# A transformer block with routed experts: softmax maxima and inverses taken off TensorE in the joined stage

## What is computed

```python
x = x + 0.5 * ffn(layernorm(x), ...)
x = x + recurrence(layernorm(x), ...)
x = x + 0.5 * ffn(layernorm(x), ...)

def ffn(x):                      # each of its two parts is residual
    h = layernorm(x) * ln1_w + ln1_b
    q, k, v = split(h @ w_qkv)   # 16 heads of 8 channels
    attn = softmax(q @ k.T / sqrt(8))
    x = x + (attn @ v) @ w_proj
    g = layernorm(x) * ln2_w + ln2_b
    e = argmax(g @ gate_w + gate_b)          # one of 8 experts
    return x + gelu(g @ w1[e]) @ w2[e]
```

## Time and profile before

| | |
|---|---|
| time, median of 3 runs | 1472.45 us (1472.34 to 1479.55) |
| the profiled execution | 1473.18 us, span 1471.4 us |
| TensorE matmul busy | 1230.9 us, 84% |
| VectorE busy | 1042.9 us, 71% |
| ScalarE busy | 860.7 us, 58% |
| GpSimd busy | 553.6 us, 38% |
| mean granted TensorE clock | 0.909 of full |

### The profile page before, as it was taken

How to read it: one execution, slowest core, us unless ns; L and a number is a source line. 1 busy time by engine, 2 the same in 40 slices (tenths; PEclk the granted TensorE clock), 3 DMA queues, 4 the chain that set the end, 5 groups by cost and what they waited for, 6 DMA issues and landing times. The chain is left out here.

```text
span 1471.4 us, 36051 instructions
## 1 busy us (share of the span) xinstructions
PE 1230.9 (84%) x12512; PEld 661.3 (45%) x12513; DVE 1042.9 (71%) x1842; ACT 860.7 (58%) x1742; POOL 553.6 (38%) x797
## 2 busy tenths in 40 slices
PE   2799999999997596398888754999999999993893
PEld 1234444444443596145455442344444444442893
DVE  3889988988992332478788745888898988963232
ACT  2288877778775353444334411588788778881451
POOL 6122324323212354355676536222332431222462
PEclk9599999999999799599999955799999999996896
DMA  4322442222110121100000003122122122100224
GB/s 117 71 74 74 130 121 68 82 71 73 55 36 9 53 67 47 42 2 3 3 2 2 3 1 87 57 75 65 49 82 73 53 81 66 56 15 30 56 66 122
DMA packets 81540, 82.40 MB, mean 56 GB/s; under 512 B 16249, under 2 KB 53724, under 8 KB 81392
## 3 DMA queue, kind: packets, MB, share of 16 engines
q1 hardware_dynamic: 72560, 69.88, 16.7%
q0 software_dynamic: 4608, 8.44, 1.8%
q10 hardware_dynamic: 4224, 2.10, 0.5%
HBM read 50.42 MB, written 29.93 MB: 55 GB/s over the span
## 5 line engine op out<-in xcount | busy, mean ns | idle before, releaser
L986 DVE TENSOR_REDUCE maxima<-ps 128x2 f32<-128x1024 f32 x512 | 616.2, 1222 | 89.8 <-PE ps L652 88.5
L933 ACT ACTIVATE probs<-ps 128x512 f32<-128x512 f32 x1024 | 550.8, 600 | 120.3 <-PE ps L660 109.7
L652 PE MATMUL ps<-k_stack,q_stack 62*128 62x512 f32 x1024 | 390.0, 473 | 39.0 <-DVE maxima L986 21.7
L660 PE MATMUL ps<-q_stack,k_stack 64*128 64x512 f32 x1024 | 396.3, 464 | 4.2 <-ACT q_whole L869 3.4
L670 PE MATMUL ps<-probs,v_stack 128*32 128x256 f32 x4096 | 329.6, 394 | 0.9 <-ACT probs L933 0.4
L652 PEld LDWEIGHTS ps<-k_stack,q_stack 62*128 62x128 f32 x1024 | 160.1, 194 | 235.9 <-issue 138.3
L660 PEld LDWEIGHTS ps<-q_stack,k_stack 64*128 64x128 f32 x1024 | 159.2, 187 | 30.5 <-ACT q_whole L869 8.6
L670 PEld LDWEIGHTS ps<-probs,v_stack 128*32 128x32 f32 x4096 | 81.7, 108 | 166.6 <-issue 148.3
L532 POOL CAST neg_wide<-maxima 128x16 fp32r<-128x16 f32 x64 | 12.6, 196 | 286.7 <-DVE maxima L986 286.7
L1299 POOL DMA_INDIRECT expert_out<-yt,number x80 | 78.3, 979 | 72.4 <-POOL number L1295 44.1
L1276 DVE COPY w_now<-w 128x512 f32 x80 | 34.6, 433 | 80.1 <-issue 42.2
(11 more groups left out here) (208 smaller groups left out, 1622.7 us busy)
## 6 DMA issues: line engine op xcount, KB each, us to landing
q_stack<-q_split SPq DMA_DIRECT2D x256, 64.0 KB
k_stack<-k_split SPq DMA_DIRECT2D x512, 32.0 KB
q_split<-q_parts SPq DMA_DIRECT2D x16, 512.0 KB, 2.7
k_split<-k_parts SPq DMA_DIRECT2D x16, 512.0 KB, 3.6
xt<-sorted SPq DMA_DIRECT2D x80, 64.5 KB
w<-in_L_ffn_w SPq DMA_DIRECT2D x16, 256.0 KB, 3.0
rows<-expert_out SPq DMA_DIRECT2D x16, 256.0 KB, 4.5
x_all<-in_L_attn_x SPq DMA_DIRECT2D x8, 256.0 KB, 5.1
```

The costliest lines, as they stand in the source:

```text
L652: mm = t.matmul(psS[:, h, :], qs[g][score_rows(h), h // 2, u * P:(u + 1) * P], ks[g][score_rows(h), h // 2, :], start=True, stop=True)
L660: t.matmul(ring("e", G, u, n), ks[G % NG][half(h), h // 2, u * P:(u + 1) * P], qs[G % NG][half(h), h // 2, :], start=True, stop=True).then ...
L933: a.activation(probs[u % 2][:, h, :], ring("e", G, u, n), ACT.Exp, scale=float(DK) ** -0.5).then_inc(e_read, 1)
L986: v.tensor_reduce(maxima[G % 2][:, :, pair, u:u + 1], psS[:, 2 * pair:2 * pair + 2, :], AX_X, ALU.max, negate=True).then_inc(s_read, 1)
```

## The change

In the joined stage:

1. The maxima. VectorE turns the 128x32 tile of a step's maxima in 32x32 blocks (`turn_maxima`, in unit 0 of the step before, after the first reduction). GpSimd splits the turned tile, SP stores both parts to a DRAM image and reads them back into the query stack: four transfers where there were two. `turn_max` and `keep_rows` are gone.
2. The products. They are not turned any more. SP moves the eight rows of sums out of oT (`move_sums`), VectorE inverts them, SP stores them and reads them back spread over 16 partitions each (`store_inv`, `spread_inv`), and GpSimd multiplies oT as it stands into one of two yT (`normalize`). The projection takes the two halves with rearranged weights: 16 pieces for 8. `turn_o`, `copy_o`, `turn_y` and `keep_y` are gone. `keep_o` waits for `o_done` of the count before.
3. The norms. zn and the normed rows are made by ScalarE, 128x128 each, with a scale and a shift that GpSimd makes (`norm_second` in (1,2) and (1,3), `norm_rows` in (3,2) and (3,3), ahead of the exponentials). `norm_first` is two wide operations, `halve` is two wide operations on GpSimd.
4. The eight jobs left stand in other units; scatter stands in g = 3 in place of g = 1. `turn_h`, `gate` and `rank` of a batch come two batches later, so that after the last value product those of two batches are to be made.
5. q and k are stored doubled in DRAM (four transfers of 512 KB a batch for two), and a group is loaded by 4 transfers for 12.
6. Six of the eight loads of x and the eight routing constants are issued in the joined stage (`load_early`), no more in the first block. The low parts of batch 0 come ahead of memsets on VectorE. Half of the padding stores are issued by ScalarE.

```diff
         def jobs(b, g, u):
             here = []
...
+            if b >= 2 and (g, u) == (0, 1):
+                here.append(("turn_h", b - 2))
+            if b >= 2 and (g, u) == (0, 3):
                 here.append(("gate", b - 2))
+            if b + 2 < B and (g, u) == (2, 0):
+                here.append(("turn_z", b + 2))
+            if b >= 1 and (g, u) == (2, 1):
+                here.append(("project", b - 1))
+            if b + 2 < B and (g, u) == (2, 2):
+                here.append(("q", b + 2))
+            if b >= 2 and (g, u) == (2, 3):
                 here.append(("rank", b - 2))
+            if b + 2 < B and (g, u) == (3, 0):
                 here.append(("k", b + 2))
             if b + 2 < B and (g, u) == (3, 2):
                 here.append(("v", b + 2))
...
+        AFTER = [(k, B - 2) for k in ("turn_h", "gate", "rank")] + [(k, B - 1) for k in ("project", "turn_h", "gate", "rank")]
...
                 def place(G):
-                    sp.wait_ge(rows_kept, G + 1)
+                    if G:
+                        sp.wait_ge(rows_placed, PLACED * G)
+                    image = max_images[G % 2]
+                    for a, ready in enumerate((split_step, split_done)):
+                        sp.wait_ge(ready, G + 1)
+                        sp.dma_start(image[a].rearrange("c k q -> k c q"), neg_parts[:, a, :].bitcast(F32)).then_inc(max_stored, 16)
+                    sp.wait_ge(max_stored, STORED * (G + 1))
                     for e in range(2):
...
                         sp.dma_start(qs[G % NG][at:at + SPLITS, :, :].bitcast(F32),
+                                     image[:, e * count:(e + 1) * count]).then_inc(rows_placed, 16)
...
                 for b, g in steps_in_order:
                     G = NG * b + g
+                    if g % SHARE and G > 1:
+                        store_inv(shared(b, g - 1))
                     if G < LAST:
                         place(G + 1)
+                    if g % SHARE == 0 and G:
+                        move_sums(shared(b, g))
+                    if g % SHARE and G > 1:
+                        spread_inv(shared(b, g - 1))
...
                 def normalize(count):
+                    n = (count - 1) % (NG // SHARE)
+                    pool.wait_ge(inv_spread, 16 * count)
+                    pool.wait_ge(projected, (count - 1) // (NG // SHARE))
+                    g_.tensor_tensor(yT[n][:], oT[:], inv_wide[:], ALU.mult).then_inc(o_done, 1)
...
                 for b, g in steps_in_order:
                     G = NG * b + g
+                    if G < LAST:
+                        split_max(G + 1)
+                    if g % SHARE == 0 and G > SHARE:
+                        normalize(shared(b, g) - 1)
                     if G and (b, g) < (B - 1, 1):
                         pool.wait_ge(pv_unit, TPB * G)
                         stage((G - 1) // NG + 1, (G - 1) % NG)
+                    if g == 1 and b + 2 < B:
                         scale(b + 2)
+                        norm_first(b + 2)
+                    if g == 3 and b >= 1:
                         row_scale(b - 1)
+                    if g == 3 and b + 2 < B:
+                        low_part(b + 2, "q")
+                        low_part(b + 2, "k")
+                    if g == 3 and b >= 2:
                         scatter(b - 2)
+                    if g == 3 and b >= 1:
+                        halve(b - 1)
+                normalize(NG * B // SHARE - 1)
+                scatter(B - 2)
+                normalize(NG * B // SHARE)
...
                 def keep_o(count):
                     act.wait_ge(pv_unit, TPB * SHARE * count)
                     if count >= 2:
-                        act.wait_ge(o_turned, count - 1)
+                        act.wait_ge(o_done, count - 1)
                     a.activation(oT[:], psO, ACT.Copy).then_inc(o_kept, 1)
...
+                def norm_second(j, tiles):
+                    act.wait_ge(shift_made, j + 1)
+                    act.wait_ge(turned, j)
+                    for q in tiles:
+                        last = a.activation(zn[:, q, :], x_all[:, j * ST + q, :], ACT.Identity, bias=shift[j % 2][:, q:q + 1],
+                                            scale=scales[j % 2][:, 1, q:q + 1])
...
                 for b, g in steps_in_order:
                     for u in range(TPB):
+                        for pair in range(PAIRS):
+                            if G + 2 <= LAST:
                                 reduce_pair(G + 2, u, pair)
+                            if (u, pair) == (0, 0) and G < LAST:
+                                turn_maxima(G + 1)
+                        if u == 0 and g % SHARE and G > 1:
+                            invert(shared(b, g - 1))
+                        if (g, u) == (0, 3) and b >= 2:
+                            choose(b - 2, b + 2 if b + 2 < B else None)
...
+                        if (g, u) == (1, 0) and b + 2 < B:
                             moments_of(b + 2)
+                        if (g, u) == (2, 1) and b >= 1:
                             add(b - 1)
+                        if (g, u) == (2, 3) and b >= 2:
+                            places(b - 2, b - 1)
...
+                        if (g, u) == (3, 0) and b >= 1:
+                            row_moments(b - 1)
```

More of the change, by code:

```diff
@@ L707, in value @@
                     last.then_inc(made["v"], 1)
-                def turn_y(p):
-                    pe.wait_ge(o_done, NG // SHARE * (p + 1))
-                    ring_free("turn_y", p)
-                    for q in range(ST):
-                        last = t.transpose(ring("turn_y", p)[:, q * P:(q + 1) * P], rows[:, p * ST + q, 0:P], s["ident"][:])
-                    last.then_inc(y_turned, 1)
                 def project(p):
@@ L928, in _ @@
                             number()
+                        if b + 2 < B and (g, u) in ((1, 2), (1, 3)):
+                            norm_second(b + 2, range(2 * u - 4, 2 * u - 2))
+                        if b >= 1 and (g, u) in ((3, 2), (3, 3)):
+                            norm_rows(b - 1, range(2 * u - 4, 2 * u - 2))
                         for n, h in enumerate(E_ORDER):
@@ L936, in _ @@
                 for kind, j in AFTER:
+                    if (kind, j) == ("turn_h", B - 1):
+                        norm_rows(j, range(ST))
                     job(kind, j)
+                act.wait_ge(pads_ready, 1)
+                for e in range(E // 2, E):
+                    row = act.value_load(pad_row[0:1, e:e + 1], min_val=0, max_val=E * (TOK + P) - P)
+                    act.dma_start(xs[ds(row, P), :], s["padding"][:, 0, :]).then_inc(act_padded, 16)
+                act.wait_ge(act_padded, 16 * (E - E // 2))
             @block.vector
@@ L1090, in _ @@
                 for j in range(2):
-                    norm_both(j, range(ST))
+                    norm_second(j)
+                for k in "qk":
+                    low_part(0, k)
                 for i in range(2):
@@ L1144, in _ @@
-                halve(B - 1)
-                norm_rows(B - 1)
-                choose(B - 1)
-                places(B - 1)
+                row_stats(B - 1, range(ST))
+                row_moments(B - 1)
+                choose(B - 1, None)
+                places(B - 1, None)
                 counted = run[SL % 2]
                 vec.wait_ge(ranks_read, SL)
-                vec.wait_ge(halved, SL)
                 v.tensor_copy(pad_row[:], counted[:]).then_inc(pads_ready, 1)
```

402 lines of the change are left out of this document (175 added, 227 removed).

## The result

The changed kernel takes 1497.2 us (median of 4 runs, 1494.8 to 1501.4) against 1472.4 us for the kernel before on the same chip (4 runs, 1471.4 to 1479.6). The ratio is 1.0161, with a 95% interval from 1.012 to 1.020: slower by 1.6%. The profiled executions are 1494.8 us (span 1493.0) and 1473.2 us (span 1471.4), so the traces have to explain 21.6 us.

The account below looks back on a forecast made before the run. TensorE, busy 50.99 of a batch's 52.2 us, was taken to bound the joined stages. From 1473.18 us, +28 for batches, +19 for tails and -17.3 for the prologue gave 1502.9, as a median 1502; range 1463 to 1534.

Parts of the forecast that it names:

- the jobs: TensorE's work between units: turns worth 2.65 us a batch removed, eight projection pieces (1.16) added, net -1.5 us.
- The old stalls: TensorE's stalls in a middle batch before the change, 3.5 of 52.2 us, all counted as removed.
- oT in (0,1): Value products wait for the single oT behind GpSimd's normalize: 1.4 us, or 2.8 to 3.1 in batches 3 to 6.
- oT in (2,1): The same wait for normalize in unit (2,1), which begins 0.59 us later behind turn_z: 0.9 us.
- Norms on ScalarE: Norms ahead of exponentials stall TensorE: 2.8 us a batch around norm_second (1.6 without VectorE's lag), 0.4 and 0.35 for norm_rows.
- Sum of a stage: Batches of one joined stage together: +13.8 us, with +3.1 each in batches 3 to 5; twice that +28.
- Tail: Last value product to next phase: add +12.6 us, norm +0.7, less 3.8 from padding stores; +9.5 a stage.
- The split of the padding stores: Eight padding stores, 8.46 us on SP, go over two queues; 3.8 us a stage come back.
- Prologue: Start of the kernel: work begins 7.3 us earlier, and each stage's start is about 5 us shorter; -17.3 us.
- (b): Rival, slower still: the maxima's way through DRAM misses odd steps' start by 1 to 2 us; 1530 us, chance 0.16.
- (c): Rival, faster: GpSimd is early, the waits fall into slack and a batch is PE-bound; 1438 us, chance 0.15.
- (d): Rival, no change: some new waits are shorter, a batch gains +0.8 us for +3.1; 1480 us, chance 0.17.

Follow-up runs that it names:

- GpSimd on time: The changed kernel (one oT, norms on ScalarE) with halve alone moved from step 3 to step 0 of the next batch: 1485.8 us.
- the fastest kernel: The changed kernel with two oT, norms on VectorE, the last normalize ahead of the scatters and halve in step 0 of the next batch: 1452.2 us.
- the tail run: The changed kernel with the last normalize ahead of batch 6's scatters and all eight padding stores on SP again: 1490.9 us.
- the edit in the kernel before: The kernel before with only the later loads of x and the routing's constants moved from the first block to the joined stage: 1463.9 us.
- the hop: The changed kernel with a 16 KB DRAM to DRAM copy between the stores and reads of the maxima in every step: 1523.0 us.
- the first three together: The changed kernel with two oT, both norms on VectorE and the last normalize ahead of the scatters, padding stores left split: 1482.8 us.

## Why the prediction came out, and where it was wrong

The forecast, 1502, is 5 us above the measured 1497, and its mechanism (in-order waits on GpSimd and ScalarE eat more than TensorE saves) is what the runs show. The sum is nearer than its terms, and that is luck. Against the profiled execution (forecast +29.7, measured +21.6) the batches came out 10.3 us below their forecast, the tails 5.1 above, the prologue 1.1 above, and 3.6 us less come from code that the change doesn't touch. The runs take a middle batch apart, one thing less in each: changed 53.4 to 55.1 us; with GpSimd on time 53.0 to 53.3; with two oT 51.8; with the norms off ScalarE too 50.7; before 52.2.

**TensorE, right.** Forecast -1.5 us a batch for the jobs. Read each job as the distance from its start to the next start on TensorE: they sum to 9.25 us in the old batch of the earlier trace rows and to 7.6 in the changed one (254.60 to 308.00), so -1.7. The sixteen units are taken at 2.46 us, 39.4 in all, in both.

**The old stalls, counted as gone and still there.** What is left of a batch after its units and jobs is 3.55 us before, as the prediction had it. It counted these 3.5 as removed. The same subtraction leaves 6.4 us in the changed batch, 4.85 with two oT (251.99 to 303.77), and 3.8 in the fastest kernel (247.53 to 298.25), where no wait of oT and no norm on ScalarE is left. So the jobs went and the stalls beside them stayed. The waits view names only a part of them. For TensorE over the old batch it has these two lines:

```profile
PE ps L652 <- DVE maxima L986: 0.8, 1, 0.8
PE ps L660 <- ACT q_whole L869: 0.3, 1, 0.3
```

The same view of the changed kernel, from 254.60 to 308.00:

```profile
PE ps L715 <- POOL v_stack L574: 1.3, 1, 1.3
PE ps L697 <- DVE maxima L1005: 0.8, 2, 0.5
PE ps L705 <- ACT probs L945: 0.3, 1, 0.3
PE ps L705 <- ACT k_whole L890: 0.3, 1, 0.3
```

The 1.1 us that the view named are there again, and so is what it doesn't name. An example of the latter in the kernel before: the value products at 253.22 and 255.74 stand 2.52 us apart, 1.93 without the 0.59 of turn_h between them, where the pace is 1.23 (a unit has sixteen value products, in two groups of eight, so two such distances). TensorE's rows show no idle time there. What holds each of these places, ScalarE's copies or VectorE's small operations, no run separates.

**oT in (0,1), right in kind, size off.** The forecast stall of the value products is 1.4 us; TensorE stands 0.96 to 1.1 with GpSimd on time (ScalarE, ahead of it, 1.19). GpSimd was to be 3.8 us late and is 2.5: its queue ends at 257.14 (split's start) where step 0 began at 254.60. Most of that is the variance, forecast at 5.5 us of step 3: its power starts at 245.97, 4.7 us into the step (241.26). What the lateness adds was given as 1.4 to 1.7 us and measures 0.35 on TensorE. Lateness counts only beyond the point where the turned maxima hold split anyway: with halve away GpSimd stands 1.84 us for them, and split starts 2.18 us into the step (202.02) for 2.54. Missing from the forecast is the clock: it knew the gate's eight pieces behind an idle stretch in the tail (1.87 us, at a granted clock of 0.50), and priced the projection there at their pace (3.8 us forecast, 3.79 measured), but took no such price for a gap of 1.5 us within a batch. It costs some 1.5 us in 4 of 14 batches, and by luck stands in for part of what was counted too high.

**oT in (2,1), wrong.** Forecast 0.9 us; ScalarE waits 0 to 0.26 us before oT there in batches 1 to 5. The turn of z stands ahead of (2,1), and ScalarE's copy hT behind it covers the same time:

```profile
229.19 1.28 POOL L592 TENSOR_TENSOR yT<-oT,inv_wide 128x512 f32<-128x512 f32 x1
...
229.68 0.78 ACT L880 ACTIVATE hT<-ps,ln_b,ln_w 128x512 f32<-128x512 f32 x1 [0.30 <-PE ps L725]
```

hT ends at 230.46, yT at 230.47: the wait is over when ScalarE comes to it. The prediction followed TensorE's order through that unit and forgot that ScalarE has the same job in its queue. Batch 6, which has no turn of z, bears this out: there oT waits 1.19 us (392.38).

**Norms on ScalarE, half wrong.** The wait for shift is there (0.70 us, forecast 1.4), and two activations take 0.88 us (forecast 0.72). But a run of stalls, worked unit by unit to 2.8 + 0.75 us, is worth 1.1. The 2.8 held the lag of VectorE behind choose, and that stays when the norms leave ScalarE; it is one of the old stalls under another name. That the banks let other delays overlap is likely, but no run shows it.

**Sum of a stage.** Forecast +13.8, measured +9.4 and +7.9. Two errors with opposite signs left it near. The prediction put all stalls of a middle batch at 8.05 us, 7.45 of them new ones of oT and the norms. The changed batch has 6.4 (some 1.5 more where the clock falls): 1.6 go with the second oT, 1.1 with the norms, and 3.8 stay. So the new ones were put at more than twice their size, and the 3.5 old ones at nothing. With one of the two corrected alone the time would have come out 50 us off or more.

**Tail.** Forecast +9.5, measured +12.1. Up to add +12.6 was forecast and +11.2 measured; the norm +0.7 forecast, +0.5 measured. The split of the padding stores failed outright: -3.8 forecast, +0.5 measured from slot to the first tile. The step said that the scatter would then end last, and took the stores for what bounded the end before. The next phase's loads start 7.4 us behind the last scatter's issue before (485.79 to 493.21) and 8.0 after (494.92 to 502.89), 7.1 in the tail run with all eight stores on one queue. The end of the stores' issue lies 3.4 us ahead of the loads in the two kernels with one queue and 8.8 in the changed one. That the scatter's landing sets this point everywhere fits these numbers; shown is only that the split gains nothing.

**Prologue, right.** -7.3 forecast and -7.4 measured, and shown alone by the edit in the kernel before; -5 each for the rest, -4.5 and -4.3.

**The rivals.** (b) was near: its cover of 1.3 us lies within what the hop finds in step 1 (0.4 to 1.7), and 2.1 to 2.9 us more on the way cost 26 us, about its price. It didn't happen because the reads landed in time: packets under 512 B went from 16249 to 38777 without TensorE in the changed kernel ever waiting for q_stack behind max_image. What such a store costs against a larger one no run here shows. (c) and (d) asked for waits that fall into slack; the run with two oT shows what they would have given, 1465 us, and that the slack was one buffer short.

**What stays open.** The experts and the recurrence between the stages, code that the change doesn't touch, are 3.6 us shorter after. From the first expert product to the second stage's first copy oT it is 460.2 us before (455.9 with the prologue's 4.3 taken off), 451.8 after, 454.6 with two oT, 456.0 with halve moved alone in the changed kernel: kernels with the same code there differ by 4.2 us. TensorE's granted clock changes level many times in that stretch (means of 0.50 to 1.00 over windows of 23 to 40 us, from 490 to 883 before and from 502 to 885 after), and it may be that it falls in other places; no run settles it.

## What to carry to other kernels

A single buffer between a producer and a consumer on two engines can make the producer wait for whatever stands ahead in the consumer's queue: before the one oT, ScalarE stood 28.2 us in 21 waits for GpSimd's yT in the changed kernel, and a second buffer of 2 KB a partition was worth 32 us here. A short gap can cost more than its length, if the granted clock falls behind it (to 0.66 behind 1.47 us here, worth some 1.5 us more): look at the clock of the stretch behind each gap. Where a step is moved to an idle engine, ask what runs beside it, not only how busy that engine is: the same 2.3 us of GpSimd cost nothing in step 0 and 30 us beside VectorE's norms in step 3. And count a stall as removed only if you know what releases it and the change takes that away: the 3.5 us a batch that were counted as gone were still there, 3.8, in the fastest kernel, and the waits view names 1.1 of them.

## What the runs showed of the hardware

**VectorE's norms were slower while GpSimd's halve ran.** Two norms of 128x128 from SBUF to SBUF took 0.60 us alone and 2.2 to 2.7 beside halve, and moving halve restored 0.59 (191.19 and 194.74 in the run that moves halve alone, with norms on VectorE). In the run with both norms back the slow pair, begun at 200.19, ends at 202.90, 0.08 us behind the end of halve's second product (202.82), and GpSimd's own operations kept their length (1.05, 1.28). The long reductions from PSUM beside the same kind of GpSimd operation kept theirs (two in 2.44 us from 201.43 in the changed kernel, the second beside yT at 202.59). GpSimd's scatters beside the norm did no harm (0.60 at 196.64, one scatter from 196.90). What in the two operations holds the norm up no run separates. In these runs halve on GpSimd and the norms on VectorE went together without loss only in different steps, and the change avoided the clash by taking the norms off VectorE.

**TensorE's granted clock fell behind a part of the gaps of 1.3 us and more in an otherwise full stretch.** Where oT waited 1.2 to 1.3 us in (0,1), TensorE itself stood 0.95 to 1.1 us, and the granted clock never fell (26 places in four kernels, 14 of them with halve moved alone). Where oT waited 1.5 us or more, TensorE stood 1.3 to 1.5 us (up to 2.7 in the hop's run), and the clock fell in 4 of 10 places in the changed kernel, 2 of 10 in the tail run and 5 of 10 in the hop's. Behind the gaps of 1.7 to 2.0 us of the run with the first three together it fell in 9 of 10. A fall, to a mean of 0.66 to 0.68 over the 5 us behind the gap, cost some 1.5 us in the changed kernel. The gap's length alone doesn't decide: in the hop's run the clock fell behind 0.59 us at 271.92 and stayed behind 1.97 us at 1296.94, and with both norms back on VectorE it fell behind 0.96 us at 150.62. What else does, no run separates.

**A load that spreads a small DRAM image over the partitions** (256 KB written) took 4.0 us from issue to use in the tail run (465.64 to 469.65), twice what the prediction took from the landing of a constant. **The 128x32 turn in 32x32 blocks** takes 0.20 us on VectorE, as estimated:

```profile
228.43 0.20 DVE L1013 STREAM_TRANSPOSE max_turned<-maxima 128x32 f32<-128x32 f32 x1
```
